# A recurrent, gated and low-rank layer chain on one core: output gate's products paired, the low-rank bias sum and its subtraction moved, the last block's sums re-dealt

## The reference

```
h[t] = tanh(h[t-1] @ Wh + x[t] @ Wx + b);            x += h       # 1 RNN, h[-1] = cond
i,f,o,g = x[t] @ Wx + h[t-1] @ Wh + b                             # 2 LSTM, h[-1] = c[-1] = cond
c = sig(f)*c + sig(i)*tanh(g); h = sig(o)*tanh(c);   x += h
out = sum_e w[b,e]*mask[e,t]*(gelu(x@ew1[e]+eb1[e])@ew2[e]+eb2[e])  # 3 top 2 of 4 experts,
      + gelu(x@sw1+sb1)@sw2+sb2;                     x += out     #   F = 1024, and a shared one
w = gelu(LN(cond)@W1+bias1)@W2 + bias2  -> a1,b1,a2,b2 (rank 8)   # 4 adapter: weights per batch
mid = gelu(x@base_down + (x@a2)@b2.T);  x += mid@base_up.T + (mid@b1)@a1.T
```

## Time and profile before

| | |
|---|---|
| median of 3 runs | 1149.6 us (1147.82 to 1151.15) |
| the profiled execution | 1146.71 us |
| its span, first to last instruction | 1144.9 us |
| busy: TensorE, weight loads, VectorE, ScalarE, GpSimd | 96, 88, 70, 53, 35% |
| TensorE clock granted, mean | 0.970 |

### The profile page before, as it was taken

How to read it: one execution, slowest core, us unless ns; L and a number is a source line. 1 busy time by engine, 2 the same in 40 slices (tenths; PEclk the granted TensorE clock), 3 DMA queues, 4 the chain that set the end, 5 groups by cost and what they waited for, 6 DMA issues and landing times. The chain is left out here.

```text
span 1144.9 us, 57020 instructions
## 1 busy us (share of the span) xinstructions
PE 1098.0 (96%) x22970; PEld 1004.3 (88%) x22970; DVE 803.9 (70%) x3194; ACT 601.1 (53%) x2147; POOL 395.3 (35%) x1372
## 2 busy tenths in 40 slices
PE   5789999999999999999999999899999999999998
PEld 4789898899899898999999998688888888888877
DVE  6576767767777776777776766687666666667697
ACT  4455666665565665665666554433333333334476
POOL 4654444445444444554555540171000000000031
PEclk8759999999999999999999999899999999999999
DMA  8301102102102200000000111000000000000022
GB/s 252 92 25 59 59 23 59 59 23 60 58 23 59 59 23 13 23 22 19 18 4 22 16 15 17 2 2 2 1 2 2 2 2 1 2 4 2 3 85 82
DMA packets 54924, 37.06 MB, mean 32 GB/s; under 512 B 25560, under 2 KB 53514, under 8 KB 54668
## 3 DMA queue, kind: packets, MB, share of 16 engines
q1 hardware_dynamic: 54060, 33.12, 10.2%
q10 hardware_dynamic: 608, 0.30, 0.1%
HBM read 28.42 MB, written 4.98 MB: 29 GB/s over the span
## 5 line engine op out<-in xcount | busy, mean ns | idle before, releaser
L1352 PE MATMUL bank<-LH,seq 128*128 128x16 f16 x8192 | 282.2, 170 | 17.8 <-DVE LH L899 17.6
L1352 PEld LDWEIGHTS bank<-LH,seq 128*128 128x128 f16 x8192 | 244.2, 96 | 30.2 <-DVE LH L899 23.5
L605 ACT ACTIVATE gel<-bank,seq 128x256 f32<-128x256 f32 x256 | 121.5, 475 | 214.7 <-PE bank L1241 211.0
L1239 PE MATMUL bank<-XHL,WE 128*128 128x256 f16 x768 | 210.7, 274 | 6.8 <-DVE XHL L849 2.7
L1239 PE MATMUL bank<-GH,WE 128*128 128x256 f16 x768 | 209.7, 273 | 1.6 <-DVE GH L862 1.2
L1241 PE MATMUL bank<-XHL,WE 128*128 128x256 f16 x768 | 210.9, 275 | 0.0
L1240 PE MATMUL bank<-XHL,WE 128*128 128x256 f16 x768 | 210.7, 274 | 0.0
L1240 PE MATMUL bank<-GH,WE 128*128 128x256 f16 x768 | 209.8, 273 | 0.0
L1241 PE MATMUL bank<-GH,WE 128*128 128x256 f16 x768 | 209.7, 273 | 0.0
L1358 PE MATMUL bank<-LH,seq 128*128 128x16 f16 x4096 | 176.9, 169 | 0.0
L565 ACT ACTIVATE tfig<-bank 128x96 f32<-128x96 f32 x256 | 66.9, 261 | 196.2 <-PE bank L1358 195.2
(11 more groups left out here) (205 smaller groups left out, 2506.1 us busy)
## 6 DMA issues: line engine op xcount, KB each, us to landing
stage<-in_L_cond_ew SPq DMA_DIRECT2D x64, 128.0 KB, 2.4
stage<-in_L_cond_W SPq DMA_DIRECT2D x32, 256.0 KB, 3.6
XHL<-in_x SPq DMA_DIRECT2D x8, 512.0 KB, 9.1
out<-WE SPq DMA_DIRECT2D x16, 256.0 KB, 2.1
stage<-in_L_cond_sw SPq DMA_DIRECT2D x2, 1024.0 KB, 5.6
scratch<-rows SPq DMA_DIRECT2D x96, 8.0 KB, 2.3
stage<-in_L_cond_Wx SPq DMA_DIRECT2D x1, 1024.0 KB, 8.7
stage<-in_L_cond_Wh SPq DMA_DIRECT2D x1, 1024.0 KB, 10.9
```

The source lines that it names most:

```text
L605: nc.scalar.activation(gel[:, m % 2, :], banks[m % len(banks)][:, 0:256], ACT.Gelu_apprx_tanh, scale=scale, bias=bias).then_inc(s["a_g"], 1)
L1239: MM(out_, w(HI), x(HI), start=start, stop=False, skip_group_check=True)
L1352: MM(z, LW[:, h, 1, c, tile * P:(tile + 1) * P], LH[:, old, HI, c], start=False, stop=False, skip_group_check=True)
```

## The change

The output gate's 12 matmuls of 16 columns become 4 of 16 columns (LO weight, HI state) and 4 of 32 (HI weight, both halves of the state). The second half lands in the other half of the bank `OB`, whose seed grows to a whole bank, with zeros from the new columns of `gate_bias`. VectorE adds the two halves (`oz`, a new reduction between `ig` and `c2`), and ScalarE takes `to` from `oz`, in `lstm_cell` ahead of `tc`, no longer in `lstm_gates`.

The bias sum goes from step 14 to step 13 of a matrix block. The LO part goes from step 15 to steps 2 and 4 of the next block, one half each. In the last block, each `cut_sums` of four reductions is dealt over two steps, later entries move, and the logits on TensorE move from step 11 to 12.

```
-        gate_bias = sb("gate_bias", [P, 8], F32)
+        gate_bias = sb("gate_bias", [P, 8 + C], F32)
+        oz = sb("oz", [P, C, B], F32)
...
-                sp.wait_ge(s["v_lowlo"], Q * C)
+                sp.wait_ge(s["v_lowlo"], Q * C * len(LO_LATER))
...
+            nc.gpsimd.memset(gate_bias[:, 8:8 + C], 0.0).then_inc(s["p_gate_bias"], 1)
...
-                act.wait_ge(s["pe_o"], n + 1)
-                nc.scalar.activation(to[:].rearrange("p (m b) -> p m b", m=C), OB[u // G][:, 0:C * G * B].rearrange(
-                    "p (m t b) -> p m t b", m=C, t=G)[:, :, u % G, :],
-                    ACT.Tanh, scale=0.5 / S_LSTM)
 
             def lstm_cell(blk, u):
                 n = blk * U + u
+                act.wait_ge(s["v_oz"], n + 1)
+                nc.scalar.activation(to[:], oz[:].rearrange("p m b -> p (m b)"), ACT.Tanh, scale=0.5 / S_LSTM)
...
-                    seed(it * U, OB[1], slice(6, 8), G, "a_o_seed")
+                    seed(it * U, OB[1], slice(6, 8 + C), G, "a_o_seed")
...
                 V.scalar_tensor_tensor(ig[:], ti, 1.0, tg, ALU.add, ALU.mult).then_inc(s["v_ig"], 1)
+                dve.wait_ge(s["pe_o"], n + 1)
+                V.reduce_sum(oz[:], OB[u // G][:, :].rearrange("p (a m t b) -> p m t b a", a=2, m=C, t=G)[:, :, u % G],
+                             AX_X).then_inc(s["v_oz"], 1)
...
-            def cut_sums(h):
+            def cut_sums(h, ks):
...
-                for k, (lo, hi_) in enumerate(spans):
+                for k in ks:
+                    lo, hi_ = spans[k]
...
-            extras = {2: seg_sums, 3: lambda: cut_sums(HI), 4: lambda: cut_sums(LO), 5: seg_sums2, 7: means,
-                      8: means2, 9: modulation, 10: last_weights, 1: silu_cond}
+            extras = {2: seg_sums, 3: lambda: cut_sums(HI, (0, 1)), 4: lambda: cut_sums(HI, (2, 3)),
+                      5: lambda: cut_sums(LO, (0, 1)), 6: lambda: cut_sums(LO, (2, 3)), 7: seg_sums2, 8: means,
+                      9: modulation, 10: means2, 13: last_weights, 1: silu_cond}
...
-                    if matrix and u == LO_WINDOW:
-                        low_lo(it - 1)
+                    if 1 < it <= 2 * E + 1 and u in LO_LATER:
+                        low_lo(it - 2, LO_LATER.index(u))
...
+                for i, tile in enumerate(O_TILES):
+                    for c in range(C):
+                        MM(o[:, 0, i], LW[:, LO, 1, c, tile * P:(tile + 1) * P], LH[:, old, HI, c],
+                           start=False, stop=False, skip_group_check=True)
+                for i, tile in enumerate(O_TILES):
+                    for c in range(C):
+                        last = MM(o[:, :, i], LW[:, HI, 1, c, tile * P:(tile + 1) * P], LH[:, old, :, c],
+                                  start=False, stop=(c == C - 1), skip_group_check=True)
+                last.then_inc(s["pe_o"], 1)
...
-                    elif u == 11:
+                    elif u == 12:
                         logits()
...
-ADD_WINDOW, HI_WINDOW, LO_WINDOW = 14, 14, 15
+ADD_WINDOW, HI_WINDOW, LO_LATER = 13, 14, (2, 4)
```

More of the change, by code:

```diff
@@ L207, in build_program @@
             a_xr p_xr pe_rx pe_r v_rz a_rh  p_rlo p_x1 p_x1h p_x1l
-            ld_gate_bias p_gate_bias a_fig_seed a_o_seed pe_fig pe_o a_fig v_ig v_c2 a_tc v_hh v_h2 v_hl v_x2
+            ld_gate_bias p_gate_bias a_fig_seed a_o_seed pe_fig pe_o v_oz a_fig v_ig v_c2 a_tc v_hh v_h2 v_hl v_x2
             pe_h a_g v_gh v_gl pe_d v_y
@@ L581, in seed @@
                 n = (tiles.stop - tiles.start) * steps * B
-                act.wait_ge(s["p_gate_bias"], 3)
+                act.wait_ge(s["p_gate_bias"], 4)
                 nc.scalar.activation(bank_[:, 0:n].rearrange("p (m t) -> p m t", t=steps * B),
@@ L591, in seeds @@
                 if u == O_SEEDS[0] and it > 0:
-                    seed(it * U, OB[1], slice(6, 8), G, "a_o_seed")
+                    seed(it * U, OB[1], slice(6, 8 + C), G, "a_o_seed")
                 if u == O_SEEDS[1] and not last:
-                    seed(it * U + G, OB[0], slice(6, 8), G, "a_o_seed")
+                    seed(it * U + G, OB[0], slice(6, 8 + C), G, "a_o_seed")
             def x_hi(blk, c):
@@ L997, in add_bias, with low_lo @@
                 V.tensor_tensor(low_f[:], low_bank, low_bias[:], ALU.add).then_inc(s["v_low"], 1)
-            def low_lo(g):
+            def low_lo(g, k):
                 dve.wait_ge(s["a_low"], g + 1)
-                part_ = lambda h: rows[:, h, bass.ds(g, 1)].rearrange("p o r d -> p d (o r)")
-                V.scalar_tensor_tensor(part_(LO), low_f[:].rearrange("p (d r) -> p d r", r=R), S_LOW, part_(HI),
+                d = slice(k * LOW_D // 2, (k + 1) * LOW_D // 2)
+                part_ = lambda h: rows[:, h, bass.ds(g, 1)].rearrange("p o r d -> p d (o r)")[:, d]
+                V.scalar_tensor_tensor(part_(LO), low_f[:].rearrange("p (d r) -> p d r", r=R)[:, d], S_LOW, part_(HI),
                                        ALU.mult, ALU.subtract).then_inc(s["v_lowlo"], 1)
@@ L1344, in lstm_step @@
                 fig = [tile_at(FIG[u // H % 2], H, i, tile) for i, tile in enumerate(FIG_TILES)]
-                o = [tile_at(OB[u // G], G, i, tile) for i, tile in enumerate(O_TILES)]
+                o = OB[u // G][:, :].rearrange("p (a m t b) -> p a m t b", a=2, m=C, t=G)[:, :, :, u % G]
                 if not isinstance(n, int) or n > 0:
                     pe.wait_ge(s["v_hh"], n)
[L1348 to L1360, removed]
@@ new lines, in lstm_step @@
+                for z, tile in fig:
+                    for c in range(C):
+                        for h in (HI, LO):
+                            MM(z, LW[:, h, 1, c, tile * P:(tile + 1) * P], LH[:, old, HI, c],
+                               start=False, stop=False, skip_group_check=True)
+                if not isinstance(n, int) or n > 0:
+                    pe.wait_ge(s["v_hl"], n)
+                for z, tile in fig:
+                    for c in range(C):
+                        last = MM(z, LW[:, HI, 1, c, tile * P:(tile + 1) * P], LH[:, old, LO, c],
+                                  start=False, stop=(c == C - 1), skip_group_check=True)
@@ new lines, in lstm_step @@
+                last.then_inc(s["pe_fig"], 1)
+                for i, tile in enumerate(O_TILES):
+                    for c in range(C):
+                        MM(o[:, 0, i], LW[:, LO, 1, c, tile * P:(tile + 1) * P], LH[:, old, HI, c],
+                           start=False, stop=False, skip_group_check=True)
+                for i, tile in enumerate(O_TILES):
+                    for c in range(C):
+                        last = MM(o[:, :, i], LW[:, HI, 1, c, tile * P:(tile + 1) * P], LH[:, old, :, c],
+                                  start=False, stop=(c == C - 1), skip_group_check=True)
```

## The result

| | before | after |
|---|---|---|
| median of 4 runs each, same chip | 1150.38 us (1147.82 to 1151.77) | 1122.11 us (1120.68 to 1123.61) |
| ratio, 95% interval | | 0.9757 [0.9734, 0.9780] |
| the profiled execution, its span | 1146.71, 1144.9 us | 1123.61, 1121.8 us |

Direction and mechanism held, the size did not: the recurrence of a step grew by 0.02 us, not by the 0.05 of the forecast.

What follows compares the result with a forecast made beforehand. TensorE and the recurrence were taken to be within 0.05 us per step of each other. Terms -13.0 + 1.0 - 0.7 - 1.6 - 2.5 + 0.8 - 0.3 = -16.3 us took 1146.71 to 1130.4, plus 2.9: 1133.3 us, range 1125 to 1145.

Steps and rivals of the forecast that it cites:

- TensorE's saving: Each step: four loads and matmuls fewer, 0.10 us per step, up to 26 us if TensorE alone set the pace.
- The recurrence's cost: Each step: `oz` and `to` start `tc` 0.05 us later, so the recurrence grows from 2.46 to 2.51 us.
- the prediction's own factor: Some 210 steps set by the recurrence, so each 0.01 us in its cost is 2.1 us.
- rival A: LSTM step: `to` delays nothing, `c2` alone releases `tc` (+0.02 us); 6 us less, 1127 us; chance 0.14.
- Rival B: LSTM step: VectorE doesn't start `c2` until `oz` has left it; +27 us, 1160 us; chance 0.07.
- The seam: End of matrix blocks: `low_hi`'s wait and `low_lo` leave, a quiet block's seam remains; -1.62 x 8 = -13.0 us.
- The halves of `low_lo`: Steps 2 and 4: halves of 0.68 us each, late by 0 to 0.18 sixteen times; +1.0 us taken.
- Rival C: Halves of `low_lo` don't fit, 0.3 us late sixteen times, and `oz` costs 0.08; 1143 us; chance 0.15.
- D: Seam: the stalls came from some other wait, so the move gives half; +6.5 us, 1140 us; chance 0.05.
- Steps 0 and 1: Block start: TensorE waits in step 1 for the split `XHL`; fewer matmuls only lengthen this wait, gain 0.
- Block 15: Last block: halved sums fit the idle time of four steps, -1.0, longer recurrence +0.7; together -0.3 us.
- The offset: From the profiled execution to the runs' median: 2.9 us added to 1130.4, giving 1133.3 us.

Runs made afterwards that it cites:

- unpaired: The changed kernel with the output gate's paired products made one by one again, `oz` and the late tanh kept: 1132.02 us, ratio 0.9851 to the kernel before.
- low_only: The kernel before with only the low-rank moves (bias sum to step 13, LO part to steps 2 and 4 of the next block): 1134.47 us, ratio 0.9867.
- oz_twice: The changed kernel with the reduction `oz` made twice in a row, the second into a tile nobody reads: 1148.27 us, ratio 0.9990 to the kernel before.
- swap_seam: The changed kernel with two pieces of the `XHL` split moved to step 15 and `add_y` from there to step 0 of the next block: 1121.85 us.
- spread_seam: The changed kernel with the output gate's seed at step 1, split pieces at steps 15 and 0, `add_y` at step 1 of the next block: 1118.28 us.
- to_late: The kernel before with only the output gate's tanh `to` moved to just ahead of `tc`, still reading the bank: 1146.92 us, ratio 0.9971.
- no_redeal: The changed kernel with only the last block's sums and the logits' step back where they were: 1124.35 us, ratio 0.9777 to the kernel before.
- oz_first: The changed kernel with `oz` ahead of `fc` instead of between `ig` and `c2`: 1130.40 us, ratio 0.9832 to the kernel before.

## Why the prediction was right in kind and 11 us short

**TensorE's saving: right.** Four matmuls fewer, and a paired one takes the 0.025 of a single one; taken back (`unpaired`), all 10 us of the gate part are gone. The weight loads of one step, block 11: 0.10 from group to group of four, with 16 columns (L1368), with 32 (L1372) and with 16 again (L1322).

```profile
506.73 0.17 PEld L1368 LDWEIGHTS bank<-LH,seq 128*128 128x128 f16 x4
506.83 0.17 PEld L1372 LDWEIGHTS bank<-LH,seq 128*128 128x128 f16 x4
506.93 0.17 PEld L1322 LDWEIGHTS bank<-RH,seq 128*128 128x128 f16 x4
```

**The recurrence's cost: the step that failed.** It is the term "2.46 + 0.05 = 2.51": the measured steps are 2.475 to 2.49. The 0.05 itself is right where it was read (`tc` starts 0.49 after `ig`). But the term stopped at the start of `tc`. Two things behind and ahead of it gave most back: `tc`, which now starts while `to` still runs, is shorter; and `tfig` comes 1.100 after the first load instead of 1.113, as it also did in the kernel before in the steps into which TensorE came waiting (5, 7, 11, 13 and 15 of a quiet block). Step 11, from which the prediction took its 2.46, was one of these; its `fc` to `ig` took 0.13 where 0.11 is usual, so it was no measure of the others. The group of `tc` in the list by line of both kernels, first before, then after (mean ns behind the busy time):

```profile
L576 ACT ACTIVATE tc<-c 128x32 f32<-128x32 f32 x256 | 58.7, 229 | 42.0 <-DVE c L895 39.3
```

```profile
L576 ACT ACTIVATE tc<-c 128x32 f32<-128x32 f32 x256 | 55.2, 216 | 0.0
```

For steps 10, 12 and 14, 2.456 long before: 2.456 + 0.047 - 0.013 - 0.013 = 2.477 where 2.475 is the least measured: +0.02. By the prediction's own factor 0.03 x 210 is 6 us, and the block lengths show it: the quiet blocks 10 to 14 gained 0.48 to 0.62 where 0.23 were forecast (0.05 in steps 3 to 15, 0.18 in step 2), 14 blocks x 0.3 = 4.2 us; block 0 lost 0.2 where 0.8 were forecast. This is rival A's size but not its mechanism: `to` does delay `tc`. A further part: the prediction read the recurrence from one step and took 2.514 as its level with TensorE, while the steps differ from 2.46 to 2.56; TensorE's long steps (2.53 to 2.56) were the ones that gained most.

**Rival B: wrong**, as weighed. `c2` follows a reduction of 0.22 after 0.13, and so does the second reduction in `oz_twice`. By the rule of the Trainium skill (VectorE: DVE Perf Modes, "The DRAIN you can't avoid") it would have started after the reduction's end, and the time would have been near rival B's 1160; this trace disagrees for this pair, and the page itself lets an operation that isn't held start earlier.

**The seam: right in the blocks, too small in the time.** -1.62 x 8 = -13.0 was forecast, the lengths of matrix blocks in `low_only` give 1.56 x 8 = 12.5, the times 15.3. What is missing is likely the clock falls that went with the stalls. The prediction named falls as a danger of the change and did not see that the kernel before already had one, in block 9.

**The halves of `low_lo`: too dear.** +1.0 was forecast; steps 3 and 5 of matrix blocks are as long as those of quiet ones (2.49). Rival C fell with it, and D with the seam.

**Steps 0 and 1: right for the wrong reason.** Their sum is 5.34 before and after. In step 0 TensorE had been 0.08 late, that is gone, and step 1 is longer by as much, since VectorE's list from `hh` of step 0 through both pieces of the split to `fc` of step 1 decides. `swap_seam` and `spread_seam` show it. Step 2 came out as forecast (2.69 to 2.49, `to_late` 2.46).

**Block 15: too little.** -0.3 was forecast, -2.6 came. Steps 4 and 5 lasted 3.01 each and are 2.48: -1.06, as forecast. Step 11, with the logits and `last_weights`, fell from 2.82 to 2.48, which the prediction had no term for, and the longer recurrence cost 0.02 to 0.03 in a few steps (+0.7 was forecast); step 9 was 3.41 in the profile before, with a clock fall, and 2.48 after. That one is luck of the single profile: `no_redeal` against the changed kernel gives 2.2 us for the sums.

**The offset.** The sum was made against 1146.71 and 2.9 was added for the median. But that execution was faster than all four timed runs of the kernel before (median 1150.4), while the profiled one of the changed kernel is its slowest. From profile to profile the gain is 23.1 us; blocks 0 to 15 gained 25.3, the start-up lost 2.3, which the prediction had no term for (block 0 begins at 45.68, not 43.39, although the clock granted until then was higher, 0.93 against 0.82). In one profile each, block 0 begins at 44.4 to 45.7 in the nine kernels with the gate part and at 43.1 to 44.9 in the six without, so part of it may be the change's; the cause stays open. Of the 11.2 us missed, 4.4 lie in the offset and 6.8 in the profile: about 4.2 + 0.6 the recurrence's term in blocks 1 to 14 and 0, 1.0 the halves of `low_lo`, 1.0 a clock fall in block 9 and 2.3 block 15, against 2.3 of start-up that were lost and some rounding.

## What to carry to other kernels

Where two engines are within a few hundredths of a microsecond per step of each other, follow the whole chain of the recurrence to the next step's start, not only to the first instruction that the change delays: its followers may shorten again, and each 0.01 us in a step counts some 200 times. Small work that an engine can do while it waits for its own result (here a reduction between `ig` and `c2`) is nearly free there and dear one place earlier. Long elementwise work at a seam belongs one piece to a step, and a profile of one run must be set against the spread of the runs before an offset is added.

## What the runs showed of the hardware

- A matmul of 32 moving columns takes TensorE no longer than one of 16: 0.025 us from load to load either way. A step's output gate streams 192 columns before and after, so the gain is that of four fewer instructions.
- VectorE takes the next operation 0.13 after the start of a reduction that lasts 0.21 to 0.22, and 0.10 to 0.11 after one of its products of 32 columns (0.18 to 0.19).
- `tc`, 32 columns from SBUF, lasts 216 ns where it starts 0.14 behind the start of `to`, and 229 where nothing ran any more when it started (the kernel before, `oz_first`, and `oz_twice`, where it starts as `to` ends); `to`, now the one that waits, 231.
- In blocks 1 to 14 the granted clock fell to 0.50 behind 8 of the 24 seams of the three kernels with two stalls there, at a cost of about 1 us each, and nowhere in the twelve others, one profile each.
